# Two-layer cross attention on one core: the first norm of x moved to GpSimd, the last tile's end in halves, and a new written order

## Chip, cores and metric

One core of a Trainium2 chip. The metric is the device time of one execution in microseconds (us), median of several runs. 0.3% of this kernel is 1.0 us.

## What is computed

x is 16 tiles of 128 tokens by 256, the context 16 tiles of 128 by 192, all in fp32. Two layers follow each other, both with 16 heads of 16 columns:

```python
# layer 0
q = layernorm(x, ln1) @ Wq;  k, v = split(layernorm(ctx, ln2) @ Wkv)
x = x + softmax(q k^T / 4) v @ Wproj + bproj
x = x + gelu(layernorm(x, ln3) @ W1 + b1) @ W2 + b2        # 256 -> 1024 -> 256
# layer 1
q = rotate(rmsnorm(x) @ wq);  k, v = split(ctx @ wkv);  k = rotate(k)
x = x + softmax(4 * unit(q) unit(k)^T) v @ wout
```

Each tile attends to its own context tile alone. Products are kept near fp32 accuracy by splitting an operand into a rounded part (`hi`) and the remainder (`lo`), and adding three products.

## The kernel before

The kernel is written for each engine by itself: one list of calls for TensorE (`pe`), VectorE (`dve`), ScalarE (`act`), GpSimd (`pool`) and SyncE (`sp`), unrolled over tiles t (0 to 15) and pairs of tiles p. Each engine works through its list in the written order. The calls are small functions (`statistics(3)`, `keys_a(1, bank_y)`) that wait on semaphores and issue one to a few instructions; between them TensorE's list has further waits for the PSUM banks. Eight banks exist: four score banks (`banks_s`) and `bank_o`, `bank_y`, `bank_t`, `bank_qk`, which all other results pass through.

**Loads.** SyncE loads x and context of tiles 0 and 1 (`load_x`, `load_ctx`, L243 to L249), then waits for the layer-0 key and value weights (`wkv_loaded`, L255), which ScalarE's queue loads in three transfers after the small vectors and Wq (L567 to L571). Then SyncE loads tiles 2 and 3, bproj and Wproj, and the later tiles; `load_x(t)` waits until tile t-4 is normalised.

**Stage A, layer-0 attention (about 13 to 140 us).** Per tile: `statistics` on VectorE (four instructions, L2198 to L2208), `inverse_std` on GpSimd (four, L318 to L331, one a power of -0.5), then `normalise` on VectorE for x (L2210 to L2216) and `normalise_context` on ScalarE (L597). Per pair: TensorE transposes (`rows_T`, `context_T`, four each), ScalarE and VectorE split (`rows_hi`/`rows_lo`, `context_hi_a`/`context_lo_a`), TensorE multiplies (`queries_a` 12 matmuls, `keys_a` and `values_mm_a` 10 each), ScalarE copies out (`queries_out_a`, `keys_out_a`, `values_out_a`). Per tile again: keys are masked in two halves (`masked_first` on ScalarE, `masked_second` on GpSimd, L354), and the scores are made twice in the same four banks. First scores (`scores_a`, L1216, 16 matmuls) serve the row maxima (`maxima`, L2233, VectorE); these are split, transposed and spread (`maxima_hi`, `maxima_lo`, `maxima_T`, `maxima_rows`). Turned scores (`scores_turned`, L1234, 16 matmuls, and `shifted`, L1243, four) overwrite the banks with the maxima taken off, and ScalarE takes the exponentials (`exps_a`, L659, two halves). TensorE then weights the values (`weighted_first`, `weighted_second`, 16 short matmuls each), ScalarE copies (`out_T`), TensorE transposes back (`back`), VectorE divides (`heads_out`), and transposes, splits, `project` (six matmuls) and `residual` end the tile. First scores of tile t+1 are made before the turned scores of tile t. `residual_bias` on GpSimd adds bproj to x once x is normalised.

**Head.** TensorE makes bias products from the raw weights (`query_bias`, `kv_bias`, `proj_bias`), with unused transposes between (`idle`). VectorE copies them out (`kv_bias_out`); `keys_out_a(0)` and `values_bias` wait for that.

**Later.** From about 140 us the MLP (`up_b`, L1326, `down_b`, L1337) runs with layer 1's keys and values mixed in, from 262 us layer 1's attention. `split_wkv`, `w1_lo_part`, `w2_hi_part`, `w2_lo_part` and `context_hi`/`context_lo` on GpSimd prepare operands. The last tile ends with `weighted(31)`, `out_T(31)`, `back(31)`, `heads_out(31)`, `normed(31)`, `out_hi(31)`, `out_lo(31)`, `project(31)`, `residual(31)` and its store.

## Time and profile before

| | us |
|---|---|
| runs | 341.33, 341.97, 341.09; median 341.33 |
| profiled execution, its own time | 343.29 |
| its span on the core | 341.5 |
| TensorE matmul busy | 330.3 (97%) |
| VectorE / ScalarE / GpSimd busy | 266.7 / 230.6 / 193.2 |
| mean granted TensorE clock | 0.992 of 2.4 GHz |

The span is the profiled part of one execution; 1.8 us of its time lie around it. Engines overlap, so their busy times don't add up. PE is TensorE's matmuls, PEld its weight loads, DVE VectorE, ACT ScalarE, POOL GpSimd, SP SyncE; SPq and ACTq are issues of transfers by SyncE and ScalarE. An arrow `<-` between tiles reads output from input; in brackets stands how long the engine was idle before and what released it. A matmul group's printed time includes the last one's way through the array, so the next group starts before it ends.

### The profile page before, as it was taken

How to read it: one execution, taken by the hardware profiler on the slowest of the kernel's cores; microseconds unless marked ns; L12 is line 12 of the kernel's file. 1: busy time of each engine (PE TensorE's matmuls, PEld its weight loads, DVE VectorE, ACT ScalarE, POOL GpSimd, SP SyncE). 2: the span in 40 equal slices, each digit the busy share in tenths (PEclk: the TensorE clock that was granted, in tenths of full speed). 3: DMA queues.
4: the chain of work that ended last, by engine and by line, in shares of the span. 5: the costliest groups of instructions: out<-in, count | busy, mean ns of one | idle time of the engine just before them, and what ended most of it. 6: DMA issues, size and time to landing. Idle time of an engine off the chain costs nothing.

```text
span 341.5 us, 10106 instructions
## 1 busy us (share of the span) xinstructions
PE 330.3 (97%) x3929; PEld 295.5 (87%) x3929; DVE 266.7 (78%) x586; ACT 230.6 (68%) x422; POOL 193.2 (57%) x200
## 2 busy tenths in 40 slices
PE   7899999999999999999999999999998999999995
PEld 7877876888778887899999999999998998888884
DVE  2969989988998669778788788666579989887643
ACT  3568876787775653885736665655678867789871
POOL 3585675886542202635857987493662799647100
PEclk9899999999999999999999999999999999999998
DMA  5667411110020000100000010000000000010101
GB/s 155 200 207 234 138 33 31 33 34 2 3 94 2 3 3 2 33 3 0 3 31 2 0 33 3 31 2 32 2 2 0 3 2 33 17 36 33 50 33 63
DMA packets 13007, 13.79 MB, mean 40 GB/s; under 512 B 1440, under 2 KB 12192, under 8 KB 12960
## 3 DMA queue, kind: packets, MB, share of 16 engines
q1 hardware_dynamic: 12240, 12.34, 11.4%
q10 hardware_dynamic: 720, 0.80, 0.8%
q8 instruction: 32, 0.52, 0.7%
q14 instruction: 15, 0.12, 0.1%
HBM read 11.04 MB, written 2.10 MB: 38 GB/s over the span
## 4 chain that ended last, share of the span: by engine, by line
PE 81%; DVE 6%; issue 4%; POOL 3%; ACT 2%; DMA 1%; ACTq 1%; POOLq 0%; DVEq 0%
PE banks_s L1326 12%; PE bank_y L1121 5%; PE banks_s L1216 5%; PE banks_s L1234 4%; PE banks_s L1393 4%; PE bank_o L1121 4%; PE bank_t L1337 4%; PE bank_y L1337 3%; PE bank_t L1121 3%; PE bank_o L1135 2%; PE bank_y L1135 2%; PE bank_o L1266 2%; PE bank_qk L1337 2%; PE bank_o L1337 2%; DVE row_max L2233 2%
## 5 line engine op out<-in xcount | busy, mean ns | idle before, releaser
L436 POOL TENSOR_TENSOR norm_q_inv<-norm_q_min,minus_half 128x32 f32<-128x32 f32 x8 | 43.8, 5476 | 21.0 <-DVE norm_q_min L2416 19.4
L424 POOL TENSOR_TENSOR norm_k_inv<-norm_k_min,minus_half 128x32 f32<-128x32 f32 x8 | 44.5, 5566 | 12.8 <-DVE norm_k_min L2383 12.7
L659 ACT ACTIVATE PT<-banks_s 128x1024 f32<-128x1024 f32 x32 | 31.0, 1023 | 15.7 <-PE banks_s L1243 15.7
L2233 DVE TENSOR_REDUCE row_max<-banks_s 128x8 f32<-128x1024 f32 x32 | 37.6, 1218 | 4.3 <-PE banks_s L1216 4.0
L703 ACT ACTIVATE W_s<-banks_s,small_t 128x256 f32<-128x256 f32 x60 | 25.2, 471 | 20.1 <-PE banks_s L1326 20.0
L1326 PE MATMUL banks_s<-lnT_hi,W_hi 128*128 128x256 f32 x120 | 34.4, 287 | 0.0
L1326 PE MATMUL banks_s<-lnT_hi,W_lo 128*128 128x256 f32 x120 | 33.9, 283 | 0.0
L1326 PE MATMUL banks_s<-lnT_lo,W_hi 128*128 128x256 f32 x120 | 33.9, 283 | 0.0
L685 ACT ACTIVATE PT<-banks_s 128x1024 f32<-128x1024 f32 x32 | 31.2, 1024 | 3.6 <-PE banks_s L1393 3.6
L712 ACT ACTIVATE hT_hi<-W_s 128x512 fp32r<-128x512 f32 x32 | 20.0, 632 | 15.8 <-PE bank_y L1337 10.1
L389 POOL TENSOR_TENSOR x_all<-x_all,b_row 128x256 f32<-128x256 f32 x16 | 12.4, 794 | 27.2 <-DVE b_xn L2316 25.4
L354 POOL TENSOR_TENSOR masked<-qkT,small_t 128x512 f32<-128x512 f32 x16 | 16.4, 1042 | 16.0 <-ACT qkT L634 15.4
L2327 DVE TENSOR_TENSOR hT_lo<-W_s,hT_hi 128x512 fp32r<-128x512 f32 x32 | 21.3, 688 | 3.9 <-ACT hT_hi L712 3.7
L1326 PEld LDWEIGHTS banks_s<-lnT_hi,W_lo 128*128 128x128 f32 x120 | 23.0, 191 | 0.0
L1326 PEld LDWEIGHTS banks_s<-lnT_lo,W_hi 128*128 128x128 f32 x120 | 23.0, 191 | 0.0
L1326 PEld LDWEIGHTS banks_s<-lnT_hi,W_hi 128*128 128x128 f32 x120 | 23.0, 191 | 0.0
L1216 PE MATMUL banks_s<-masked,qkT 32*128 32x256 f32 x256 | 18.3, 400 | 0.8 <-DVE row_max L2233 0.5
L1234 PE MATMUL banks_s<-masked,qkT 32*128 32x256 f32 x256 | 18.3, 400 | 0.4 <-DVE row_max L2233 0.4
L343 POOL TENSOR_TENSOR x_all<-x_all,bproj_row 128x256 f32<-128x256 f32 x16 | 11.6, 734 | 9.3 <-DVE xn L2216 9.3
L1393 PE MATMUL banks_s<-W_hi,keysT 32*128 32x256 f32 x256 | 15.6, 301 | 0.0
L1216 PEld LDWEIGHTS banks_s<-masked,qkT 32*128 32x128 f32 x256 | 11.6, 184 | 4.5 <-ACT PT L659 1.9
L1234 PEld LDWEIGHTS banks_s<-masked,qkT 32*128 32x128 f32 x256 | 11.6, 184 | 3.3 <-DVE row_max L2233 1.2
(375 smaller groups left out, 1088.6 us busy)
## 6 DMA issues: line engine op xcount, KB each, us to landing
x_all<-in_x SPq DMA_DIRECT2D x16, 128.0 KB, 2.2
ctx_in<-in_ctx_wide SPq DMA_DIRECT2D x16, 128.0 KB, 2.5
W_s<-in_L_xattn_W SPq DMA_DIRECT2D x2, 1024.0 KB, 7.8
ctx_in<-in_ctx_T SPq DMA_DIRECT2D x8, 256.0 KB, 2.6
out<-x_all SPq DMA_DIRECT2D x16, 128.0 KB, 1.7
W_s<-in_L_xattn_Wq ACTq DMA_DIRECT2D x1, 256.0 KB, 3.4
W_s<-in_L_xattn_Wkv ACTq DMA_DIRECT2D x1, 256.0 KB, 4.5
W_s<-in_L_xattn_Wkv ACTq DMA_DIRECT2D x2, 128.0 KB, 4.8
```

Of the source, the lines that this page charges most:

```text
L424: nc.gpsimd.tensor_tensor(norm_k_inv[:, :], norm_k_min[:, :], minus_half[:, :], ALU.pow).then_inc(c_kinv, 1)
L436: nc.gpsimd.tensor_tensor(norm_q_inv[:, :], norm_q_min[:, :], minus_half[:, :], ALU.pow).then_inc(c_qinv, 1)
L659: nc.scalar.activation(PT[:, t % 2, 2 * h:2 * h + 2, :], banks_s[:, 2 * h:2 * h + 2, :], ACT.Exp, scale=HD ** -0.5).then_inc(a_exped, 1)
L685: nc.scalar.activation(PT[:, t % 2, 2 * h:2 * h + 2, :], banks_s[:, 2 * h:2 * h + 2, :], ACT.Exp, scale=HD ** 0.5).then_inc(c_exped, 1)
L703: last = nc.scalar.activation(hT[:, m, :], bank[:, in_pair(k, 256)], ACT.Gelu, bias=b1_cols[:, m:m + 1])
L1121: last = mm(out, a[:, x, k, :], b[:, y, k, :], start=k == n == 0, stop=k == 1 and n == 2)
L1216: last = mm(bank_s[g][:, in_pair(k, 2 * TOK)], qkT[quad(g), p % 2, k, cols], masked[quad(g), t % MASKS, KT + k, :, :], start=True, stop=True)
L1234: mm(bank_s[g][:, in_pair(k, 2 * TOK)], qkT[quad(g), p % 2, KT + k, cols], masked[quad(g), t % MASKS, k, :, :], start=k == 0, stop=False)
L1326: last = mm(bank[:, in_pair(m % 2, 256)], w[:, k, 128 * m:128 * m + 128], act_T[:, k, :], start=k == n == 0, stop=k == KT - 1 and n == 2)
L1337: last = mm(bank[:, 0:C1], h[:, m, 128 * j:128 * j + 128], w[:, m, :], start=m == n == 0, stop=m == HM - 1 and n == 2)
L1393: last = mm(bank_s[g][:, in_pair(k, 2 * TOK)], keysT[quad(g), a, k, in_pair(t, TOK)], masked_q[b][quad(g), p % 2, k, :, in_pair(j, TOK)], ...
L2233: v.tensor_reduce(row_max[:, 8 * h:8 * h + 8], banks_s[:, 2 * h:2 * h + 2, :].rearrange("p n (r k) -> p (n r) k", k=TOK), AX.X, ALU.max).t ...
```

## The change

1. `normalise(t)` moves from VectorE to GpSimd, as one `tensor_scalar` of 128x256. `statistics(t)` on VectorE now also waits until tile t-2 is normalised.
2. The three transfers of the key and value weights move from ScalarE's queue to SyncE's, behind the loads of tiles 0 and 1.
3. For the last tile (31), the steps from the values' weighting to the projection are done in two halves of eight heads, in two banks each.
4. All engines' lists are reordered, and the four banks are given out anew.

```diff
@@ SyncE @@
             load_ctx(1)
+            sp.dma_start(Wkv_s[:, 0, :], Wkv[0:128, :]).then_inc(wkv_loaded, LOADED)
+            for half in (slice(0, C2B), slice(C2B, 128)):
+                sp.dma_start(Wkv_s[half, 1, :], Wkv[128:C2, :]).then_inc(wkv_loaded, LOADED)
             sp.wait_ge(wkv_loaded, 3 * LOADED)
@@ ScalarE @@
-            act.dma_start(Wkv_s[:, 0, :], Wkv[0:128, :]).then_inc(wkv_loaded, LOADED)
-            for half in (slice(0, C2B), slice(C2B, 128)):
-                act.dma_start(Wkv_s[half, 1, :], Wkv[128:C2, :]).then_inc(wkv_loaded, LOADED)
@@ GpSimd (removed from VectorE, where it was v.tensor_scalar) @@
+            def normalise(t):
+                j = t % 2
+                pool.wait_ge(a_rstd, t + 1)
+                pool.wait_ge(a_stats, 2 * t + 1)
+                wait(pool, a_xT, t // 2)
+                nc.gpsimd.tensor_scalar(xn[:, j, :], tile_of(t), mean_var[:, j, 0:1], rstd[:, j, 0:1], ALU.subtract, ALU.mult)\
+                    .then_inc(a_xn, 1)
@@ VectorE, statistics(t) @@
             wait(dve, a_shift, t - 1)
+            wait(dve, a_xn, t - 1)
@@ GpSimd's new list begins @@
+            inverse_std(0) normalise(0) inverse_std(1) normalise(1) inverse_std(2) normalise(2)
+            inverse_std(3) normalise(3) values_bias(0) masked_second(0) masked_second(1)
+            residual_bias(0) residual_bias(1) residual_bias(2) residual_bias(3) inverse_std(4)
+            masked_second(2) masked_second(3) normalise(4) residual_bias(4) inverse_std(5)
+            normalise(5) residual_bias(5) inverse_std(6) normalise(6) residual_bias(6)
...
@@ VectorE's new list begins @@
+            statistics(0) wq_lo_a(0) wq_lo_a(1) statistics(1) query_bias_out(0, bank_o)
+            wkv_lo_a(0) wkv_lo_a(1) statistics(2) rows_lo(0, bank_o) context_lo_a(0, bank_t)
+            statistics(3) statistics(4) wproj_lo(0) kv_bias_out(0, bank_y) statistics(5)
+            rows_lo(1, bank_o) proj_bias_out(0, bank_t) context_lo_a(1, bank_y) maxima(0)
+            maxima_hi(0) maxima_lo(0) maxima_rows(0, bank_y) maxima(1) maxima_hi(1) maxima_lo(1)
+            statistics(6) maxima_rows(1, bank_o) statistics(7) rows_lo(2, bank_y) statistics(8)
+            context_lo_a(2, bank_t) maxima(2)
...
@@ TensorE's list, head, without the waits for banks @@
-            rows_T(0) context_T(0) idle(7) queries_a(0) keys_a(0) rows_T(1) values_mm_a(0)
-            proj_bias(0) scores_a(0) context_T(1) queries_a(1) scores_a(1) keys_a(1) maxima_T(0)
-            values_mm_a(1) scores_turned(0) shifted(0) context_T(2) rows_T(2) maxima_T(1)
-            weighted_first(0) scores_a(2) weighted_second(0) queries_a(2) back(0) scores_turned(1)
+            rows_T(0) context_T(0) idle(8) queries_a(0) keys_a(0) values_mm_a(0) rows_T(1)
+            context_T(1) proj_bias(0) scores_a(0) queries_a(1) keys_a(1) values_mm_a(1)
+            maxima_T(0) scores_a(1) scores_turned(0) shifted(0) maxima_T(1) rows_T(2)
+            context_T(2) weighted_first(0) queries_a(2) scores_a(2) weighted_second(0)
+            rows_T(3) back(0) scores_turned(1)
...
@@ TensorE's list, end @@
-            weighted_first(31) weighted_second(31) project(29) normed(30) back(31) project(30)
-            normed(31) project(31)
+            weighted_first(31) weighted_second(31) project(29) normed(30) back_half(0)
+            back_half(1) project(30) normed_half(0) normed_half(1) project_half(0) project_half(1)
@@ one of the halved steps, on VectorE @@
+            def heads_half(h, bank):
+                o, part = bank[:, :].rearrange("p (h d) -> p h d", h=H), slice(H // 2 * h, H // 2 * h + H // 2)
+                dve.wait_ge(o_back, 2 * NB + h)
+                dve.wait_ge(on_ready, 2 * NB - 1)
+                v.reciprocal(row_sums_inv[:, part], o[:, part, HD]).then_inc(recip, 1)
+                dve.wait_ge(recip, 2 * NB + h)
+                dve.wait_ge(on_transposed, 2 * NB - 1)
+                v.tensor_tensor(heads(on[:, in_pair(h, TOK)], H // 2), o[:, part, 0:HD], each(row_sums_inv[:, part], H // 2, HD), ALU.mult).then_inc(on_ready, 1)
@@ VectorE's new list ends @@
+            out_lo(30) heads_half(0) heads_half(1) residual(30) out_lo_half(0) out_lo_half(1) residual(31)
```

## Rows read from the trace of the kernel before

**Rows 1.** Windows: us, busy us (instructions) per engine, TensorE clock, DMA share, GB/s

```profile
13.00:140.00 127.00, 124.41 (x1574) 100.87 (x1572) 110.76 (x255) 87.31 (x150) 69.35 (x119) 0.99 0.20 63
...
140.00:260.00 120.00, 119.31 (x1052) 117.74 (x1046) 88.96 (x177) 77.89 (x165) 80.37 (x51) 1.00 0.03 10
```

**Rows 2.** Timeline, score banks: start us, us, work [idle before <-releaser]

```profile
20.11 1.15 PE L1216 MATMUL banks_s<-masked,qkT 32*128 32x256 f32 x16
...
23.74 1.15 PE L1216 MATMUL banks_s<-masked,qkT 32*128 32x256 f32 x16 [0.47 <-DVE row_max L2233]
...
25.00 2.35 DVE L2233 TENSOR_REDUCE row_max<-banks_s 128x8 f32<-128x1024 f32 x2
...
27.51 1.15 PE L1234 MATMUL banks_s<-masked,qkT 32*128 32x256 f32 x16
...
28.97 1.92 ACT L659 ACTIVATE PT<-banks_s 128x1024 f32<-128x1024 f32 x2
...
30.94 1.15 PE L1216 MATMUL banks_s<-masked,qkT 32*128 32x256 f32 x16
...
131.36 1.15 PE L1216 MATMUL banks_s<-masked,qkT 32*128 32x256 f32 x16 [0.19 <-ACT PT L659]
```

**Rows 3.** Timeline, TensorE work between the score groups

```profile
32.58 1.70 PE L1121 MATMUL bank_y<-xT_r,Wq_r 128*128 128x256 f32 x12
...
56.00 0.63 PE L1256 MATMUL bank_o<-PT,vals 128*17 128x128 f32 x16
...
57.44 0.63 PE L1288 MATMUL bank_o<-ident,oT 128*128 128x128 f32 x4 [0.81 <-ACT oT L673]
```

**Rows 4.** VectorE groups, whole span: shapes, xcount | busy us, mean ns | idle before

```profile
L2308 DVE SCALAR_TENSOR_TENSOR b_xn<-x_all,b_mean_var,ln_rows 128x256 f32<-128x256 f32 x16 | 8.1, 545 | 2.2 <-PE bank_o L1313 2.2
...
L2216 DVE TENSOR_SCALAR xn<-x_all,mean_var,rstd 128x256 f32<-128x256 f32 x16 | 6.8, 432 | 0.0
```

**Rows 5.** Timeline, VectorE at 97 to 99 us

```profile
97.12 1.91 DVE L2308 SCALAR_TENSOR_TENSOR b_xn<-x_all,b_mean_var,ln_rows 128x256 f32<-128x256 f32 x2
...
98.95 0.68 DVE L2221 TENSOR_TENSOR xT_r<-bank_t,xT_r 128x512 fp32r<-128x512 f32 x1
```

**Rows 6.** GpSimd groups, whole span, columns as in rows 4

```profile
L389 POOL TENSOR_TENSOR x_all<-x_all,b_row 128x256 f32<-128x256 f32 x16 | 12.4, 794 | 27.2 <-DVE b_xn L2316 25.4 <-ACT qkT L634 1.8
...
L403 POOL CAST wkv_r<-wkv_s 128x256 fp32r<-128x256 f32 x4 | 1.6, 404 | 0.0
```

**Rows 7.** Timeline of the head, issues of loads and two waits

```profile
1.67 0.49 ACTq L569 DMA_DIRECT2D W_s<-in_L_xattn_Wkv  x1
...
2.12 0.43 SPq L249 DMA_DIRECT2D ctx_in<-in_ctx_wide  x1
...
11.59 0.69 PE L1129 MATMUL bank_t<-ident,xn 128*128 128x128 f32 x4 [1.19 <-DVE xn L2216]
...
11.62 0.43 SPq L249 DMA_DIRECT2D ctx_in<-in_ctx_wide  x1
...
15.00 0.43 DVE L2203 BATCH_NORM_STATS2 stats<-x_all 128x6 f32<-128x256 f32 x1 [0.19 <-DMA ctx_in<-in_ctx_wide]
```

**Rows 8.** Chain that ended last, the head: start us, us, what

```profile
2.75 4.97 DMA W_s<-in_L_xattn_Wkv
```

**Rows 9.** Busy time in windows of 1 us, columns as in rows 1

```profile
12.00:13.00 1.00, 1.00 (x8) 1.00 (x7) 1.00 (x7) 0.60 (x1) 0.57 (x3) 0.54 0.83 282
...
14.00:15.00 1.00, 1.00 (x6) 1.00 (x6) 0.81 (x2) 0.32 (x1) 0.97 (x4) 0.50 0.72 236
...
15.00:16.00 1.00, 1.00 (x9) 1.00 (x8) 1.00 (x5) 0.72 (x2) 0.20 (x2) 0.75 0.17 49
```

**Rows 10.** Timeline, end of the span

```profile
335.54 0.25 DVE L2274 RECIPROCAL row_sums_inv<-bank_o 128x16 f32<-128x16 f32 x1
...
336.97 0.39 ACT L679 ACTIVATE onT_r<-bank_o 128x256 fp32r<-128x256 f32 x1 [1.81 <-PE bank_o L1295]
...
338.94 0.42 DVE L2290 TENSOR_TENSOR x_all<-x_all,bank_o 128x256 f32<-128x256 f32 x1 [1.13 <-PE bank_o L1121]
```

More of the change, by code:

```diff
@@ new lines, in _ @@
+            pe.wait_ge(onT_lo, 14)
+            project(13, bank_o)
+            pe.wait_ge(a_max_rows, 16)
+            values_mm(1, bank_t)
+            pe.wait_ge(a_exped, 32)
+            up_b(0, 1, bank_s[0])
+            pe.wait_ge(res_ready, 14)
+            back(14, bank_o)
+            pe.wait_ge(oT_ready, 15)
+            weighted_first(15, bank_qk)
+            weighted_second(15, bank_qk)
+            pe.wait_ge(on_ready, 15)
+            normed(14, bank_o)
+            up_b(0, 2, bank_s[1])
@@ L2541, in _ @@
-            statistics(14)
-            maxima_rows(8, bank_y)
-            residual(4, bank_t)
-            normalise(14)
+            heads_out(6, bank_o)
+            rows_lo(6, bank_t)
+            statistics(15)
+            maxima_rows(8, bank_o)
+            centre_b(0)
+            residual(5, bank_qk)
             maxima(9)
-            out_lo(5, bank_qk)
+            out_lo(6, bank_o)
             maxima_hi(9)
             maxima_lo(9)
-            heads_out(6, bank_o)
-            statistics(15)
+            normalise_b(0)
@@ L2789, in _ @@
+            out_lo(21, bank_o)
             heads_out(22, bank_qk)
@@ L2805, in _ @@
             heads_out(26, bank_qk)
[L2806 to L2808 removed]
+            out_lo(25, bank_t)
+            queries_out_lo(7, bank_y)
+            residual(25, bank_t)
             heads_out(27, bank_qk)
```

1741 lines of the change are left out of this document (875 added, 866 removed).

## The prediction

> **What bounds the kernel now.** I read the stage windows first. From 13 to 140 us (the first layer's attention, "stage A") TensorE is busy 124.4 of 127 us and VectorE 110.8; from 140 to 260 us TensorE is busy 119.3 of 120 [rows 1]. So after 140 us a gain has to come from TensorE work or from the last microseconds, and stage A is where waits can go.
>
> In stage A the four score banks form a ring that I read off the timeline [rows 2]: first scores (1.15 us), maxima on VectorE (2.35), turned scores with the shift (27.51 until the exponentials start at 28.97, 1.4), exponentials on ScalarE (1.92), then the next first scores. With about 0.05 us between two steps a turn takes 7.0 us. From the first scores of tile 2 (30.94) to those of tile 15 (131.36) 13 turns took 100.4 us, 7.72 each, 9.3 us over that floor. TensorE works on other matmuls while VectorE (2.42 us with its gaps) and ScalarE (2.04) hold the banks. I priced these from starts: 12 matmuls 1.5 us, so 10 are 1.25; 16 short ones 0.5; four transposes 0.35 to 0.5 (a row's last 0.15 to 0.2 us is pipeline) [rows 3]. Added up over the written order of before, what exceeds its slot comes to 6.3 us; that is work and stays. The other 3.0 us are waits for VectorE or ScalarE.
>
> VectorE's part in them: the normalisation that is moved is 16 x 432 ns = 6.8 us; its group of two-tile reads L2308 takes 545 ns an instruction [rows 4]. At 97 us two of these took 1.91 us, 0.8 more than twice the mean, and the split of xT_r behind them started at 98.95 only [rows 5].
>
> **The change part by part.** (1) **Normalisation to GpSimd.** VectorE loses 16 x 0.43 us, 6.1 us of it in stage A, 0.4 of some 7.7 us a tile. GpSimd gains 16 instructions that no row shows. With one wide input it is nearest to the cast of 256 columns (404 ns); the two-input one of that size took 794 ns [rows 6]. I take 0.5, as it also fetches two scalars: 8 us, range 6.5 to 12.7. GpSimd is busy 69 of 127 us [rows 1], so there is room for the sum, though not at each place. New waits: statistics(t) on VectorE waits for xn of tile t-2, behind which stand maxima and all splits; rows_T waits as before, now on GpSimd's queue, where the masks and residual_bias stand too. residual_bias no longer waits for VectorE. Of the 3.0 us of waits I take back 2.0, range 0 to 3.0: VectorE's load falls from 87 to 82%, and not all waits were its.
>
> The GPSIMD Engine Reference of the Trainium skill (section 4.1) holds that elementwise work belongs on VectorE, two-input operations being about twice as slow on GpSimd and one-input ones near line rate. By its second half the moved instruction would be at the 0.43 of VectorE and the sum 0.1 to 0.2 us better at most.
>
> (2) **Weights' loads.** The three issues leave ScalarE's queue, the first at 1.67 us, and go behind SyncE's fourth at 2.12 [rows 7], so each is 0.5 to 0.7 us later. The last landed at 7.72 [rows 8]. x and context of tile 1 go ahead and land sooner, which hides nothing that waits now. If the engines' traffic sets the landing, nothing moves; if the issue does, 0.7 later. I take 0.4: 8.15. SyncE holds its next loads until then. TensorE's bias matmuls took 2.3 us behind the landing and end at 10.4 now; rows_T(0), which waited for xn until 11.59 [rows 7], starts there: xn of tile 1 (statistics at 7.0, GpSimd's reciprocal root, 0.5 us) is ready at 9.2 to 9.8. That is 1.1 us gained.
>
> (3) **The clock in the head.** TensorE waited 1.2 us for xn [rows 7], and the granted clock from 12 to 16 us was 0.54, 0.50, 0.50 (two windows alike, one stands) and 0.75, so mostly 1.2 GHz [rows 9]; before that it was full. Without the wait I take it to stay at 2.4 GHz, so queries_a(0) takes 1.5 us in place of 2.05.
>
> (4) **But what is gained is not kept to the loop.** The written order puts kv_bias_out on VectorE behind statistics(3), statistics(4) and wproj_lo(0). Context of tile 4 was issued at 11.62 and VectorE waited for it until 15.00 [rows 7]; xn now releases that load 0.4 us sooner and the weights hold it 0.4 later, so it lands at 14.9. Adding 0.9 for statistics(4), 0.65 for wproj_lo, 0.15 for the copy: 16.65. ScalarE's keys_out_a(0) 0.85, values_out_a 0.6, rows_hi(1) 0.6 and masked_first(0) 0.75 follow in its order: 19.5, first scores of tile 0 at 19.6 in place of 20.11 [rows 2]. Then all of queries, keys and values of pair 1 (1.5 + 1.25 + 1.25 us) stand between first scores 0 and 1: those of tile 1 start at 24.75 (23.74 before). Turned scores 0 follow them directly, with no work between: TensorE idles for the maxima, 2.4 us, to 28.35 (27.51 before). Exponentials to 31.75, but the first half lets weighted_first(0) run, and queries_a(2), now ahead of first scores 2, ends at 32.8: tile 2 at 32.8 in place of 30.94, **+1.86 us**, with queries_a(2) done. From there to tile 15 its excess over the slots is 5.7 us in place of 6.3, **-0.6**; the same work has then been done in both. Behind tile 14's shift one half of weighted is moved back: **-0.3**.
>
> (5) **The last tile in halves.** Before: reciprocal 335.54, product, transposes, ScalarE's copy 336.97 (0.39), VectorE's remainder, six matmuls, residual 338.94 [rows 10]. In halves the reciprocal still waits for out_lo(30) at 335.54. A half of an operation of 0.39 to 0.42 us costs about 0.28 (VectorE: 0.42 for 256 columns [rows 10], 0.68 for 512 [rows 5]). The halves follow each other at 0.3: transposes 336.45 and 336.65, copies to 337.4, remainders to 337.7, last three matmuls done at 338.4: **-0.5**, range -0.1 to -0.9.
>
> (6) **The rest of the order** (second half of the kernel, banks renamed). It moves values_mm and keys_c forward where TensorE is full anyway: 0, by the cover of 119.3 of 120 us; without it, up to 1 us either way.
>
> **Sum:** +1.86 - 0.6 - 0.3 - 2.0 - 0.5 = -1.5 us. The profiled execution took 343.29 us (span 341.5), so 341.8; it lies 2.0 above the median, and from the median of 341.33 it is **339.8 us**. A measurement here tells 0.3%, 1.0 us, from no change.
>
> **The rivals.** *GpSimd comes late, slower.* The place: normalise(4), (5), (6), behind masked_second(2) and (3) at 24 to 32 us; rows_T(2), and statistics(8) in front of the maxima of tile 2, wait on them, by my timeline with only 0.3 us to spare. At 0.8 us in place of 0.5 three of them make 0.9, less 0.3 spare: +0.6; and a VectorE that stands in a statistics wait takes none of the 2.0 back: 339.8 + 0.6 + 2.0 = 342.4. It decides from about 0.6 us an instruction. For it speaks the 794 ns, against it the 404 ns [rows 6] and GpSimd's idle time. Chance 0.23.
>
> *VectorE and GpSimd collide, no change.* The 0.8 us lost at 97 us [rows 5] fell beside a 1.5 us subtraction on GpSimd. If each of the 16 new ones costs VectorE 0.25, 4 of the 6.8 us freed are gone, and with them 1.2 to 1.5 of the 2.0: 341.2. Chance 0.14. SBUF — State Buffer of the Trainium skill (section "Who interferes with whom") gives a mechanism: a VectorE instruction with two SBUF inputs contends with a GpSimd one that reads SBUF. By that rule the row's loss is explained, and the removed normalisation, one wide input, gave way to nothing.
>
> *The clock falls in the new gap.* TensorE idles 2.4 us after tile 1's first scores, longer than the 1.2 us ahead of the low stretch [rows 7, 9]. The same stretch costs (0.46 + 2 x 0.50 + 0.25) = 1.7 us: 341.5. Chance 0.10.
>
> *All waits go.* Relief of 3.0, and the weights no later (0.4): 338.4, or 337.5 with the later stages' 0.9. Chance 0.13.
>
> **How the numbers follow.** My forecast has 0.40, its own range 338.8 to 340.8. The range 337.4 to 342.8 takes in the ends of GpSimd's price, of the landing and of part 6. Faster: three quarters of 0.40, 0.13 and a little of the rest, 0.46; same 0.23; slower 0.31.
>
> **What would show it.** Right: xn on GpSimd at 0.4 to 0.6 us; rows_T(0) near 10.4; clock 1.00 from 12 to 16 us; first scores of tiles 0, 1, 2 near 19.6, 24.8, 32.8; tile 15 near 130.3 to 131; residual to store shorter by 0.5. Wrong: xn above 0.7 us, statistics waiting for GpSimd, a half-rate stretch after 28 us, or tile 2's first scores before 31.

## The result, and the profile after

The changed kernel took a median of 351.10 us in 4 runs (348.48 to 352.84) beside 341.33 us for the kernel before: the ratio is 1.0277 with the interval 1.0207 to 1.0346. It is slower by 2.8%, where 339.8 us (337.4 to 342.8) was forecast. The profiled execution took 351.86 us with a span of 349.8, against 343.29 and 341.5. The profiled execution of the kernel before is one of its longer ones: of nine others, taken beside e17, four with a mean granted clock of 1.000 took 341.06 to 342.09 us and five at 0.992 to 0.995 took 342.01 to 342.88.

First TensorE's timeline, which answers to [rows 2] and [rows 7]: L1168 turns rows of x, L1255 is the first scores, L1273 the turned scores, L1160 the queries, L1174 the keys.

```profile
10.61 0.63 PE L1168 MATMUL bank_o<-ident,xn 128*128 128x128 f32 x4 [0.59 <-POOL xn L347]
...
24.10 1.15 PE L1255 MATMUL banks_s<-masked,qkT 32*128 32x256 f32 x16
27.72 1.15 PE L1273 MATMUL banks_s<-masked,qkT 32*128 32x256 f32 x16 [2.48 <-DVE row_max L2288]
...
30.52 1.09 PE L1168 MATMUL bank_y<-ident,xn 128*128 128x128 f32 x4 [1.05 <-POOL xn L347]
...
33.37 2.83 PE L1160 MATMUL bank_y<-xT_r,Wq_r 128*128 128x256 f32 x12
36.13 1.15 PE L1255 MATMUL banks_s<-masked,qkT 32*128 32x256 f32 x16
...
42.86 0.58 PE L1174 MATMUL bank_o<-yT_r,Wkv_r 128*128 128x256 f32 x1 [1.73 <-DVE on L2332]
...
140.11 0.50 PE L1255 MATMUL banks_s<-masked,qkT 32*128 32x256 f32 x4 [0.19 <-ACT PT L684]
```

From such starts the 8.3 us of span can be laid out. The first scores of tiles 0, 1, 2, 3 and 15 start at 18.89, 24.10, 36.13, 46.60 and 140.11 us, before at 20.11, 23.74, 30.94, 38.45 and 131.36. So the head comes 1.22 earlier; the step to tile 1 loses 1.58, that to tile 2 4.83, that to tile 3 2.96; the twelve steps from there together 0.60; and what follows tile 15's scores gains 0.45. Nearly the whole loss lies in 22 us of the span. The 1.22 of the head can't be credited to the change: e4, e7, e8, e10, e17 and e18 below have the same written order up to tile 0's first scores, and these start at 19.23 to 20.15 us there.

What became slow is one row of GpSimd's groups (columns as in rows 4), where 0.5 us had been taken:

```profile
L347 POOL TENSOR_SCALAR xn<-x_all,mean_var,rstd 128x256 f32<-128x256 f32 x16 | 20.1, 1254 | 0.0
```

Who waited for `xn`, from the view of that tile (us in all, times); in the kernel before no line of VectorE's waited for it:

```profile
who waited for it (us, times):
  ACT xT_r L633: 5.3, 6
  DVE stats L2266: 2.8, 5
```

GpSimd's timeline ahead of tile 2 (L355 is residual_bias, L334 the shift of the context's norm):

```profile
25.91 1.22 POOL L347 TENSOR_SCALAR xn<-x_all,mean_var,rstd 128x256 f32<-128x256 f32 x1
27.21 0.72 POOL L355 TENSOR_TENSOR x_all<-x_all,bproj_row 128x256 f32<-128x256 f32 x1
...
28.98 0.19 POOL L334 TENSOR_TENSOR y_shift<-minus_mean,rstd 128x1 f32<-128x1 f32 x1
29.14 1.22 POOL L347 TENSOR_SCALAR xn<-x_all,mean_var,rstd 128x256 f32<-128x256 f32 x1
```

and ScalarE's:

```profile
29.20 0.60 ACT L622 ACTIVATE yn<-ctx_in,y_shift,rstd 128x256 f32<-128x256 f32 x1 [3.27 <-POOL y_shift L334]
29.71 1.00 ACT L684 ACTIVATE PT<-banks_s 128x1024 f32<-128x1024 f32 x1
31.64 0.60 ACT L633 ACTIVATE xT_r<-bank_y 128x512 fp32r<-128x512 f32 x1 [0.93 <-PE bank_y L1168]
32.13 1.02 ACT L684 ACTIVATE PT<-banks_s 128x1024 f32<-128x1024 f32 x1
```

The two halves of tile 0's exponentials belong together, as at 28.97 in [rows 2]. Here the first stands behind a norm of the context that waits for GpSimd's shift. Of ScalarE's 3.27 us of idle time this costs the exponentials about 0.6: TensorE had the turned scores with their shift ready at 29.10 us, and the first half starts at 29.71. The second half stands behind a copy of the turned rows of pair 2, which wait for norm 5, done at 30.37 us, and starts at 32.13. The queries of pair 2 stand ahead of tile 2's first scores and take 2.83 us instead of 1.7, because the clock has fallen. The windows (columns as in rows 1) of stage A, of the next stage, and of two microseconds behind TensorE's idle stretch:

```profile
13.00:140.00 127.00, 118.81 (x1447) 94.81 (x1445) 100.89 (x224) 83.89 (x144) 80.86 (x127) 0.96 0.21 59
140.00:260.00 120.00, 119.89 (x1087) 117.33 (x1088) 90.22 (x186) 73.80 (x161) 78.40 (x55) 1.00 0.04 12
29.00:30.00 1.00, 0.46 (x5) 0.14 (x1) 0.51 (x2) 0.80 (x2) 1.00 (x2) 0.56 0.65 205
30.00:31.00 1.00, 0.48 (x3) 0.52 (x4) 0.68 (x3) 0.71 (x1) 0.92 (x2) 0.50 0.01 3
```

In stage A TensorE is busy for 5.6 us less of the same 127 us than in [rows 1]; the next stage is as full as it was. The granted clock was at half rate, 1.2 GHz, from 29.1 to 36.0 and from 42.8 to 46.2 us.

At tile 3 something else shows, on VectorE's timeline:

```profile
39.74 1.22 DVE L2299 CAST max_cols<-row_max 128x16 fp32r<-128x16 f32 x1
41.00 1.19 DVE L2304 TENSOR_TENSOR max_cols<-row_max,max_cols 128x16 f32<-128x16 f32 x1
...
42.38 0.42 DVE L2332 TENSOR_TENSOR on<-bank_o,row_sums_inv 128x256 f32<-128x256 f32 x1
```

and on GpSimd's at the same time:

```profile
39.66 3.72 POOL L372 TENSOR_TENSOR W_lo<-W_s,W_hi 128x512 fp32r<-128x512 f32 x3 [0.74 <-ACT W_hi L615]
```

The two small operations take 0.17 to 0.18 us at tile 0, with no subtraction of weights beside them. Behind them stands `on`, for which the keys of pair 2 wait until 42.86 us, ahead of tile 3's first scores.

The end, for [rows 10], on VectorE: first reciprocal of a half, and the last residual.

```profile
344.19 0.20 DVE L2344 RECIPROCAL row_sums_inv<-bank_t 128x8 f32<-128x8 f32 x1
...
347.24 0.42 DVE L2360 TENSOR_TENSOR x_all<-x_all,bank_o 128x256 f32<-128x256 f32 x1 [0.93 <-PE bank_o L1440]
```

3.05 us between these starts, against 3.40 before.

### The profile page after: what moved, and what is told of

It reads as the page before. It is cut to its first block, busy times and chain, and to the rows that moved or that the text cites. A ratio compares the mean times of both kernels' runs of the same rounds, so it can differ in the third digit from the quotient of the medians.

```text
span 349.8 us, 10121 instructions
## 1 busy us (share of the span) xinstructions
PE 333.7 (95%) x3930; PEld 296.9 (85%) x3930; DVE 264.3 (76%) x573; ACT 231.9 (66%) x424; POOL 211.4 (60%) x216
## 4 chain that ended last, share of the span: by engine, by line
PE 70%; DVE 4%; issue 2%; POOL 2%; ACT 1%; POOLq 0%; DVEq 0%; ACTq 0%
PE banks_s L1365 13%; PE bank_t L1376 6%; PE banks_s L1452 4%; PE bank_y L1376 4%; PE bank_o L1160 4%; PE bank_y L1160 4%; PE bank_o L1376 3%; PE banks_s L1273 3%; PE bank_y L1174 2%; PE banks_s L1255 2%; PE bank_o L1305 2%; PE bank_t L1160 2%; PE bank_y L1176 2%; DVE row_max L2288 1%; PE bank_qk L1305 1%
## 5 line engine op out<-in xcount | busy, mean ns | idle before, releaser
L740 ACT ACTIVATE W_s<-banks_s,small_t 128x256 f32<-128x256 f32 x62 | 26.0, 472 | 19.5 <-PE banks_s L1365 19.3
L1365 PE MATMUL banks_s<-lnT_hi,W_hi 128*128 128x256 f32 x124 | 35.4, 285 | 0.0
L1365 PE MATMUL banks_s<-lnT_lo,W_hi 128*128 128x256 f32 x124 | 35.1, 283 | 0.0
L1365 PE MATMUL banks_s<-lnT_hi,W_lo 128*128 128x256 f32 x124 | 35.1, 283 | 0.0
L2397 DVE TENSOR_TENSOR hT_lo<-W_s,hT_hi 128x512 fp32r<-128x512 f32 x32 | 22.1, 703 | 4.8 <-ACT hT_hi L749 4.5
L401 POOL TENSOR_TENSOR x_all<-x_all,b_row 128x256 f32<-128x256 f32 x16 | 12.9, 825 | 19.6 <-DVE b_xn L2386 19.6
L1365 PEld LDWEIGHTS banks_s<-lnT_hi,W_lo 128*128 128x128 f32 x124 | 23.8, 192 | 0.0
L1273 PE MATMUL banks_s<-masked,qkT 32*128 32x256 f32 x256 | 18.3, 400 | 3.4 <-DVE row_max L2288 3.3
L347 POOL TENSOR_SCALAR xn<-x_all,mean_var,rstd 128x256 f32<-128x256 f32 x16 | 20.1, 1254 | 0.0
L1255 PE MATMUL banks_s<-masked,qkT 32*128 32x256 f32 x256 | 18.3, 400 | 0.2 <-ACT PT L684 0.2
L1273 PEld LDWEIGHTS banks_s<-masked,qkT 32*128 32x128 f32 x256 | 11.6, 184 | 7.0 <-DVE row_max L2288 5.1
L1376 PE MATMUL bank_t<-W_hi,hT_hi 128*128 128x256 f32 x56 | 16.3, 291 | 0.0
L423 POOL CAST ctxT_r<-ctx_in 128x512 fp32r<-128x512 f32 x8 | 4.9, 611 | 18.4 <-issue 9.1
```

The costliest lines, as they stand in the source:

```text
L740: last = nc.scalar.activation(hT[:, m, :], bank[:, in_pair(k, 256)], ACT.Gelu, bias=b1_cols[:, m:m + 1])
L1255: last = mm(bank_s[g][:, in_pair(k, 2 * TOK)], qkT[quad(g), p % 2, k, cols], masked[quad(g), t % MASKS, KT + k, :, :], start=True, stop=True)
L1273: mm(bank_s[g][:, in_pair(k, 2 * TOK)], qkT[quad(g), p % 2, KT + k, cols], masked[quad(g), t % MASKS, k, :, :], start=k == 0, stop=False)
L1365: last = mm(bank[:, in_pair(m % 2, 256)], w[:, k, 128 * m:128 * m + 128], act_T[:, k, :], start=k == n == 0, stop=k == KT - 1 and n == 2)
L1376: last = mm(bank[:, 0:C1], h[:, m, 128 * j:128 * j + 128], w[:, m, :], start=m == n == 0, stop=m == HM - 1 and n == 2)
L2397: v.tensor_tensor(hT_lo[:, part(u), :], hT[:, part(u), :], hT_hi[:, part(u), :].bitcast(fp32), ALU.subtract)\
```

## The experiments

"Old order" is the written order of the kernel before on all engines, "new order" that of the changed one. The last columns are starts of first scores in the profiled execution, in us. Each ratio is to runs of the kernel before on the same chip, whose median was 341.31 to 342.09 us in these batches.

| run | norm of x | order | median us | ratio to before [interval] | t0 | t1 | t2 | t3 | t15 |
|---|---|---|---|---|---|---|---|---|---|
| before | VectorE | old | 341.33 | | 20.11 | 23.74 | 30.94 | 38.45 | 131.36 |
| after | GpSimd 1224 ns | new | 351.10 | 1.0277 [1.0207, 1.0346] | 18.89 | 24.10 | 36.13 | 46.60 | 140.11 |
| e1 | GpSimd 396 ns | new | 349.64 | 1.0217 [1.0173, 1.0260] | 19.47 | 24.67 | 34.53 | 44.20 | 139.56 |
| e2 | GpSimd 612 ns | new | 349.10 | 1.0199 [1.0156, 1.0242] | 19.23 | 24.43 | 33.54 | 44.07 | 138.18 |
| e3 | VectorE | new | 356.69 | 1.0415 [1.0379, 1.0451] | 19.16 | 24.37 | 34.95 | 45.55 | 144.91 |
| e4 | GpSimd 1224 | new, gap filled | 348.00 | 1.0169 [1.0145, 1.0192] | 20.12 | 25.31 | 35.44 | 42.94 | 136.81 |
| e5 | GpSimd 1224 | old | 346.17 | 1.0123 [1.0097, 1.0148] | 20.91 | 24.53 | 31.71 | 40.09 | 134.15 |
| e6 | VectorE | old, queue, halves | 342.06 | 1.0007 [0.9986, 1.0028] | 18.70 | 22.33 | 29.54 | 37.03 | 129.92 |
| e7 | GpSimd 1224 | new, w1 later | 355.62 | 1.0403 [1.0373, 1.0433] | 19.78 | 24.98 | 35.91 | 43.10 | 143.71 |
| e8 | GpSimd 1224 | new, scores first | 348.82 | 1.0205 [1.0172, 1.0237] | 19.23 | 24.43 | 33.71 | 42.94 | 136.65 |
| e9 | GpSimd 396 | old | 341.75 | 0.9998 [0.9981, 1.0015] | 18.40 | 22.02 | 29.22 | 36.71 | 129.58 |
| e10 | GpSimd 1224 | new, keys after | 352.45 | 1.0313 [1.0266, 1.0361] | 20.12 | 24.21 | 39.10 | 47.01 | 140.62 |
| e11 | GpSimd 1224 | new, e8 + e10 + w1 last | 356.83 | 1.0423 [1.0381, 1.0464] | 19.32 | 23.40 | 36.44 | 45.60 | 142.91 |
| e12 | GpSimd 396 | as e11 | 349.72 | 1.0235 [1.0198, 1.0273] | 19.01 | 23.09 | 34.38 | 43.29 | 137.69 |
| e13 | GpSimd 1224 | new, biases later | 349.18 | 1.0216 [1.0187, 1.0244] | 20.69 | 25.89 | 35.42 | 42.65 | 136.79 |
| e14 | GpSimd 1224 | e13 + turned early | 351.94 | 1.0285 [1.0250, 1.0319] | 21.94 | 27.13 | 34.17 | 43.08 | 140.65 |
| e15 | GpSimd 396 | as e14 | 348.98 | 1.0208 [1.0181, 1.0234] | 19.96 | 25.17 | 32.21 | 41.12 | 137.50 |
| e16 | GpSimd 1224 | old, biases later, queue, halves | 347.19 | 1.0173 [1.0140, 1.0207] | 19.21 | 22.84 | 30.15 | 42.11 | 135.48 |
| e17 | GpSimd 1224 | new, lists repaired | 349.96 | 1.0224 [1.0202, 1.0246] | 20.15 | 25.36 | 32.39 | 41.30 | 139.06 |
| e18 | GpSimd 1224 | e17, norms 10, 11 first | 349.18 | 1.0216 [1.0192, 1.0240] | 19.25 | 24.45 | 31.48 | 40.39 | 136.37 |

### e1 and e2: a shorter instruction in the new order

```diff
-nc.gpsimd.tensor_scalar(xn[:, j, :], tile_of(t), mean_var[:, j, 0:1], rstd[:, j, 0:1], ALU.subtract, ALU.mult)
+nc.gpsimd.tensor_copy(xn[:, j, :], tile_of(t))                                  # e1
+nc.gpsimd.tensor_tensor(xn[:, j, :], tile_of(t), <mean, broadcast>, ALU.subtract)  # e2
```

> The changed kernel, in which the normalisation on GpSimd is replaced by a plain copy of the same 128x256 tile; mean and deviation of x are left out. The trace of the changed kernel shows the moved instruction at 1254 ns, where I had taken 500; the copy should take about 0.4 us, close to my 0.5. Theory A (the instruction's length makes GpSimd late): the time falls to about 340, within 1.5 us of my forecast of 339.8, and the first scores of tile 3, at 46.6 us in the changed kernel and 38.45 before, come at 38 to 40. Rival B (the new written order costs it, above all the empty stretch behind the first scores of tile 1 and the half-rate clock after it, whatever GpSimd takes): 347 or more.

> The changed kernel, in which the normalisation on GpSimd is replaced by a subtraction of the mean alone (two inputs, one of them broadcast); the factor is left out. About 0.75 us an instruction, between the copy and the 1.25 us. Theory A: between the two, 342 to 345, nearer to the copy if GpSimd's queue has slack, nearer to 351 if it has none. Rival B: 347 or more, as the copy.

The rows of `xn` in the view of that tile (ns: least, median, most; first and last start in us), e1:

```profile
L347 POOL COPY xn<-x_all x16: 392/396/398, 7.6 to 96.2; 128x256 f32<-128x256 f32 x16
```

e2:

```profile
L347 POOL TENSOR_TENSOR xn<-x_all,mean_var x16: 608/612/617, 6.7 to 94.7; 128x256 f32<-128x256 f32 x16
```

Below the 0.5 us of the forecast, e1 is still 7.6 us slower than before. The length alone is not the cause; of the 8.75 us at tile 15 it gave back 0.55 (1.13 counted from tile 0's first scores). e2, between the two lengths, took 349.10 us. Theory A fell in both, and rival B's 347 us or more held. The intervals of e1, e2 and the changed kernel overlap, so these runs don't resolve what the length costs in this order.

### e3: the norm back on VectorE, new order

The function and its 16 calls go back to VectorE's list, at places near those of before that I chose; everything else is the changed kernel.

> The changed kernel with the normalisation back on VectorE (16 instructions of 0.43 us, placed near statistics of tile t+2 in its list); every other list, the loads' queue and the halves stay as changed. Theory A: 340 to 343, since GpSimd is relieved of 20 us and VectorE only takes 6.8 back in a list that was not made for it. Rival B: 347 or more.

With e11 this is the slowest, 14.6 us over before (342.05 in its batch), and rival B's range held. The new order thus seems to need the time that the move frees on VectorE; but the places of the 16 calls were chosen by hand, and no run tells their share from that. One norm stands out on VectorE's timeline:

```profile
25.08 1.26 DVE L2254 TENSOR_SCALAR xn<-x_all,mean_var,rstd 128x256 f32<-128x256 f32 x1
```

and beside it on GpSimd's:

```profile
24.15 2.04 POOL L357 TENSOR_TENSOR masked<-qkT,small_t 128x512 f32<-128x512 f32 x2 [0.39 <-ACT qkT L634]
```

The median of e3's 16 norms is 414 ns.

### e4: TensorE's idle stretch filled

```diff
 scores_a(1)
+pe.wait_ge(a_bp, 1)
+for n in range(22): nc.tensor.transpose(bank_t[:, 0:128], ident[:, :], ident[:, :])   # unused
 pe.wait_ge(a_maxed, 4)
```

> The changed kernel with 22 unused transposes on TensorE in the empty stretch between the first scores of tile 1 and the turned scores of tile 0. They compute nothing that is used. If the half-rate clock from 28.8 us on comes of that stretch and costs as much as I priced (1.7 us), the granted clock stays at 1.00 there and the time falls by 1 to 2 us, to 349 to 350. If GpSimd's lateness alone sets the pace (theory A), the clock may stay up but the time changes by less than 0.5 us. If they only add work: slower by up to 0.5.

Windows of e4, columns as in rows 1; against the same two windows of the changed kernel the clock stays at 1.00:

```profile
29.00:30.00 1.00, 1.00 (x21) 0.86 (x20) 0.97 (x5) 0.00 (x0) 1.00 (x4) 1.00 0.87 254
30.00:31.00 1.00, 0.57 (x9) 0.14 (x1) 0.61 (x4) 0.59 (x2) 0.92 (x3) 1.00 0.46 138
```

Useless work made the kernel 3.1 us faster, more than the 1 to 2 us expected. The step to tile 2 fell from 12.03 to 10.13 us and that to tile 3 from 10.47 to 7.50. At tile 3 the maxima's splits also no longer fell beside the weights' subtraction (they take 0.19 and 0.18 us), and e7 below shows that this alone brings the step to 7.19. So the 3.1 us are clock and collision together, and how they divide is not shown.

### e5 and e9: the move alone, old order

```diff
 # GpSimd's list of before, for each t
 inverse_std(t)
+normalise(t)
 # VectorE: its 16 calls go; in statistics(t)
+wait(dve, a_xn, t - 1)
```

> The kernel of before with one edit: the first norm of x on GpSimd, each right behind its inverse deviation, with VectorE's statistics waiting for it; the other engines' written order, the loads and the end stay those of before. Theory A (the written order of the change costs the time, not the 1254 ns on GpSimd): GpSimd's length makes a few waits near the first tiles only, 341 to 345 us, with first scores of tile 15 within 3 us of before's 131.36. Rival B (GpSimd's length holds the statistics and the turned inputs in any order): 348 us or more, first scores of tile 15 at 137 us or later.

> The kernel of the old order with the norm on GpSimd, in which the 1224 ns instruction is a plain copy of about 0.40 us (mean and deviation left out), so that only its length is changed against the old order's 346.17 us. Theory A (in the old order the move costs what the instruction is longer than the 0.5 us of the prediction): 341.5 to 343 us, within 1.5 us of before. Rival B (the two waits that the move adds, GpSimd for the turned pair and VectorE's statistics for GpSimd, cost it, whatever the length): 344.5 to 346.5 us.

e5 lies between its two theories: tile 15 is 2.79 us later, as A had it, and the time 1.2 us above A's range. e9 is A's. Together they settle the length in the old order: at 396 ns the move costs nothing that the runs can tell, at 1224 ns 4.4 us. From tile 1 to 7 e9 makes the steps of before to 0.02 us. So neither rival about the added waits as such holds; and against e1 (same instruction, new order) the new order costs 7.9 us. In these 7.9 are the queue and the halves, which e6 puts at nothing, and the banks given out anew, which no run separates from the order.

### e6: loads' queue and halves alone

The diff of the change for the three loads of Wkv and for the last tile, on the kernel before.

> The kernel of before with the loads of Wkv on SyncE's queue and the last tile's end in halves, and nothing else. The steps of the prediction put the halves at -0.5 us (-0.1 to -0.9) and the loads at 0 (-0.3 to +0.3): 340.8 us beside 341.3. If the halves' extra instructions cost what they save, within 0.2 us of before. The profile is to show the last projection's start against the last weighted product, as a check of the first, and the clock and start of the first scores for the second.

No difference that the runs can tell. In the trace reciprocal to last residual is 3.06 us (334.07 to 337.13) for 3.40, so the halves' 0.34 us is there, and it is the part of the change that does what it was forecast to.

### e7: weights' subtractions later

```diff
 inverse_std(8)
-w1_lo_part(0), (1), (2)
 masked_second(4)
 masked_second(5)
+w1_lo_part(0), (1), (2)
 w1_lo_part(3)
 normalise(8)
```

> The changed kernel with its three w1_lo_part (0 to 2) on GpSimd behind masked_second(4) and (5), as far back as part 3, so that they no longer lie beside the maxima's splits of tile 2. Theory A (the GpSimd subtractions slow the two small VectorE operations from 0.17 to 1.2 us each, and heads_out(0), keys_a(2) and first scores of tile 3 are late by that): both operations below 0.3 us, first scores of tile 3 1.5 to 2.5 us nearer to those of tile 2, 348.5 to 349.5 us. Rival B (the delay is hidden by another wait, or the half clock runs on): within 0.5 us of the changed kernel's 351.1.

Timeline of VectorE:

```profile
39.51 0.17 DVE L2299 CAST max_cols<-row_max 128x16 fp32r<-128x16 f32 x1
39.72 0.17 DVE L2304 TENSOR_TENSOR max_cols<-row_max,max_cols 128x16 f32<-128x16 f32 x1
...
52.35 0.43 DVE L2266 BATCH_NORM_STATS2 stats<-x_all 128x6 f32<-128x256 f32 x1 [3.82 <-POOL xn L347]
```

and of GpSimd:

```profile
46.01 5.00 POOL L372 TENSOR_TENSOR W_lo<-W_s,W_hi 128x512 fp32r<-128x512 f32 x4
51.00 1.21 POOL L347 TENSOR_SCALAR xn<-x_all,mean_var,rstd 128x256 f32<-128x256 f32 x1
```

Theory A's first half holds: without the subtraction beside them the splits are back at 0.17 us, and the step to tile 3 is 7.19 us for 10.47. But nothing of this is kept. Norm 8 stands behind the four subtractions in both kernels. In e7 GpSimd starts them only behind the masked copies, and norm 8 starts at 51.00 us, as in the changed kernel (50.91), while VectorE is now 3.5 us ahead. Its statistics wait 3.82 us for that norm, tile 3's splits stand behind these, and the clock is at half rate from 54.8 to 61.7 us. The kernel loses 4.5 us more and falls in neither range. The added wait of VectorE, harmless in e9, is what such a place costs.

### e8: scores ahead of queries

```diff
 # ScalarE
-rows_hi(2, bank_y)
 exps_a_second(0)
+rows_hi(2, bank_y)
 # TensorE
-queries_a(2, bank_y)
 scores_a(2)
+queries_a(2, bank_y)
```

> The changed kernel with two places of its written order exchanged: on ScalarE the second exponentials of tile 0 ahead of rows_hi(2), on TensorE the first scores of tile 2 ahead of queries_a(2). Theory A (the order makes scores of tile 2 wait for rows_T(2), rows_lo(2) and the queries, which GpSimd's norm makes late): first scores of tile 2 at 31.5 to 33.5 us instead of 36.13, and 347.5 to 350 us. Rival B (what is gained there is lost at tile 3, since the keys, maxima and clock are late all the same): first scores of tile 3 within 0.7 us of 46.60, and 350.3 to 351.5 us.

Theory A: both steps shorten (9.28 and 9.23 us), though tile 2, at 33.71 us, lies 0.2 outside its range. The median is 2.3 us lower, but the interval of the ratio just overlaps that of the changed kernel. The clock is at half rate from 27.6 to 34.4 us here too.

### e10, e11, e12: repairs that made it worse

e10 moves keys and values of pair 1 and maxima_T(0) behind scores_a(1), as in the old order, and maxima_rows(0) behind maxima(1). e11 adds e8 and puts all w1_lo_part behind residual_bias(10); e12 is e11 with the copy.

> The changed kernel with the keys and values of pair 1 and the turning of tile 0's maxima on TensorE behind the first scores of tile 1, where the old order has them, and VectorE's maxima_rows(0) behind maxima(1). Nothing else is changed. Theory A (the idle stretch at 25.2 to 27.7 us comes of the written order, and the half clock at 28.8 us of it): no half clock from 28 to 36 us, first scores of tile 2 1 to 3 us earlier than 36.13, 347.5 to 349.5 us, near the 348.0 us of the kernel in which unused transposes filled the stretch. Rival B (the turned scores of tile 0 come later by the moved work, 2 us, and take it back): 350 to 352 us.

> The changed kernel with three repairs of its written order together: keys and values of pair 1 behind the first scores of tile 1; exponentials and first scores of tile 2 ahead of rows_hi(2) and queries_a(2); all four w1_lo_part on GpSimd behind residual_bias(10). The norm stays on GpSimd at 1224 ns. Theory A (the order is what costs over the 346.17 us of the old order with the same norm): 345 to 347 us, no half clock after 28 us, maxima's splits of tile 2 at 0.17 us each. Rival B (later places of the new order cost as much by themselves): 348 us or more, with first scores of tile 15 at 136 us or later.

> The three repairs with the norm's instruction as a plain copy of about 0.40 us on GpSimd (mean and deviation left out). Theory A (order and length together are the whole loss): 341 to 343.5 us. Rival B (a remainder that neither explains, in the order of tiles 4 to 15): 344.5 us or more; first scores of tile 3 near 38.5 us and the distance from there to tile 15 (92.91 us in the kernel of before) 95 us or more.

The idle stretch ahead of tile 0's turned scores is gone, yet the step to tile 2 is 14.89 us in e10: TensorE now idles 4.11 us for norm 5, at 30.3 to 34.4, and the clock is at half rate from 34.6 to 38.0 us. Theory A of all three fell. e10 is 0.45 us above rival B's range too; e11 and e12 are in rival B's, but in e12 tile 3's first scores come at 43.29 us and not near 38.5, so the loss is not where that rival had it. The traces say why. ScalarE in e12:

```profile
31.08 0.60 ACT L622 ACTIVATE yn<-ctx_in,y_shift,rstd 128x256 f32<-128x256 f32 x1 [2.40 <-POOL y_shift L334]
31.59 1.92 ACT L684 ACTIVATE PT<-banks_s 128x1024 f32<-128x1024 f32 x2
```

and GpSimd:

```profile
26.64 2.04 POOL L366 TENSOR_TENSOR masked<-qkT,small_t 128x512 f32<-128x512 f32 x2 [3.06 <-ACT qkT L659]
28.62 0.40 POOL L347 COPY xn<-x_all 128x256 f32<-128x256 f32 x1
...
30.86 0.19 POOL L334 TENSOR_TENSOR y_shift<-minus_mean,rstd 128x1 f32<-128x1 f32 x1
```

GpSimd's list has masked_second(2) and (3) ahead of norm 4. They wait for keys 1; later keys make norm 4, then inverse deviation 5 late; ScalarE's norm of context 5 waits for its shift; and tile 0's exponentials, whose bank TensorE had ready at 28.2, stand behind that. The new order has the keys early, and GpSimd's list needs them there. e11 and e12 differ in the instruction alone: in this order 1224 in place of 396 ns cost 7.1 us.

### e13 to e16: GpSimd's list by need

e13 changes GpSimd's list alone:

```diff
 inverse_std(2)
-normalise(2)
 inverse_std(3)
+normalise(2)
 normalise(3)
...
 masked_second(1)
-residual_bias(0), (1), (2), (3)
 inverse_std(4)
+normalise(4), inverse_std(5), normalise(5)
 masked_second(2)
 masked_second(3)
+residual_bias(0) to (3), then 6 and 7 likewise
```

e14 also turns pair 2's rows and context between scores_a(1) and scores_turned(0), with their copies ahead of the exponentials, and has e8's exchange on TensorE. e15 is e14 with the copy. e16 is e13's list in the old order, with queue and halves.

> The changed kernel with one edit, on GpSimd's list alone: inverse deviations and norms of tiles 3, 4 and 5 as early as their inputs are there, and residual_bias(0) to (7), which nobody needs before the first residual sum, behind them. Theory A (GpSimd's own order is what makes the turned inputs of pair 2 late: four residual biases at 19.50 to 22.32 us and two masked copies stand ahead of norm 4, and norm 5 ends at 30.37 us): norm 5 ends by 25 us, the turned inputs of pair 2 (30.52 us) and the first scores of tile 2 (36.13 us) come 1.5 us and 2 to 4 us earlier, 346 to 349 us. Rival B (TensorE's idle stretch at 25.2 to 27.7 us and its half clock hold tile 2): 349.5 to 351.5 us.

> As the one before, and the turned inputs and context of pair 2 on TensorE in the idle stretch between the first scores of tile 1 and the turned scores of tile 0, with their splits ahead of the exponentials of tile 0 on ScalarE and VectorE, and the first scores of tile 2 ahead of queries_a(2). Theory A (the whole loss lies in tiles 1 to 3, in what TensorE waits for there): first scores of tile 2 at 30.5 to 32 us, no half clock after 28 us, 342 to 344.5 us. Rival B (each wait removed gives way to the next, as in the three repairs before): 347 us or more.

> As the one before, with the norm on GpSimd as a plain copy of about 0.40 us (mean and deviation left out). Theory A (with GpSimd's list in this order its length is covered): within 1 us of the one before. Rival B (the length still costs, as the 4.4 us between 346.17 and 341.75 us in the old order): 2 us or more below it.

> The old written order with the norm on GpSimd at 1224 ns, the loads of Wkv on SyncE's queue and the end in halves, and GpSimd's list as in the two before (norms early, residual biases late). Theory A (the 4.2 us of the norm in the old order are its places behind other work of GpSimd): 341.5 to 343.5 us. Rival B (the length itself, 1224 ns beside 432 ns on VectorE, costs): 345 to 346.5 us.

Norm 5 ends at 26.1 us in e13 (25 expected), no half clock is left, and the steps to tiles 2 and 3 are 9.53 and 7.23 us; e14's step to tile 2 is 7.04, shorter than before's 7.20. But the swap of norm 2 and inverse deviation 3 holds statistics(4) for 2.67 us, and first scores 0 come 1.80 and 3.05 us later (not all of it by the swap: e17, without it, is still 1.26 later, and so far the head scatters by itself); e14 loses another 4.1 against the changed kernel at tiles 4 and 5, where w1_lo_part stands ahead of norm 8. e15 is 3.0 us below e14: the length is not covered. By their times e13 lies between its two theories, and rival B held for e14 and e15. In e16, whose steps to tiles 1 and 2 are those of before within 0.11 us, the step to tile 3 is 11.96. At 347.19 us e16 is beyond rival B's range and 1.0 above e5, without this list. ScalarE's timeline names the place:

```profile
34.92 0.60 ACT L622 ACTIVATE yn<-ctx_in,y_shift,rstd 128x256 f32<-128x256 f32 x1 [1.36 <-POOL y_shift L334]
35.43 0.58 ACT L698 ACTIVATE oT<-bank_qk 128x512 f32<-128x512 f32 x1
```

out_T(0), for which TensorE waits 2.68 us, stands behind the norm of context 7. That one waits for inverse deviation 7 on GpSimd, which stands behind norm 6 (32.42 to 33.65 us) and, until 31.2 us, the four residual biases put ahead of it.

### e17 and e18: the places left

e17 is e14 without the swap in the head, with norms 6 to 9 ahead of biases and of w1_lo_part, and statistics 6 and 7 earlier on VectorE. e18 puts norms 10 and 11 ahead too, and w1_lo_part behind the other weights' work.

> The changed kernel with the norm on GpSimd at 1224 ns and its first 18 tile steps as they are (norm 2 ahead of inverse deviation 3 again), then GpSimd's list by need: norms 4 to 9 ahead of the residual biases and of w1_lo_part, the masked copies between; the turned inputs and context of pair 2 in TensorE's idle stretch, as in e14; VectorE's statistics 6 and 7 ahead of maxima_rows(0) and (1). Theory A (the loss of 9.1 us is places in the lists of tiles 1 to 5, above all what stands on GpSimd ahead of the norms, and the length is coverable): first scores of tile 0 near 18.9, tile 2 near 31.1, tile 3 near 39, no wait of VectorE's statistics over 1 us after 20 us, 342 to 345 us. Rival B (each wait gives way to the next one, since GpSimd has no time left beside 1224 ns a tile): 347 us or more.

> As e17, with the one place that the trace of e17 shows left: norms 10 and 11 on GpSimd ahead of all w1_lo_part, of masked_second(6) and (7) and of the first splits of wkv; three w1_lo_part behind the last w2_lo_part (GpSimd idles there from 73.6 to 78.0 us) and the last behind residual_bias(15). Theory A: the step from tile 5 to 6 falls from 12.08 to 8.3 us (8.34 in the changed kernel) without the half clock at 64 us, first scores of tile 15 at 135.3, 345.5 to 346.5 us, that is the time of the old order with this norm (346.17). Rival B (the next place takes it back): first scores of tile 15 at 138 us or later, 348.5 us or more.

e17 is 4.80 us ahead of the changed kernel at tile 5 and loses it in the next step (12.08 us), on TensorE:

```profile
63.99 0.78 PE L1168 MATMUL bank_qk<-ident,xn 128*128 128x128 f32 x4 [2.71 <-POOL xn L347]
64.70 2.09 PE L1273 MATMUL banks_s<-masked,qkT 32*128 32x256 f32 x16
```

In e18 that step is 7.95 us, as forecast; the steps to tiles 7 to 10 then take 34.23 us for 31.30 in the changed kernel, and the median, 0.8 us lower, is no difference that the runs can tell. Whether the weights' work, now in one stretch there, makes these steps long was not traced. Theory A of both fell on the total. Of its places it had e17's step from tile 0 to 2 (12.24 us for 12.2) and e18's to tile 6; e17's tile 3, at 41.30 us for 39, and e18's tile 15, at 136.37 for 135.3, it had not. The rivals' times held, though e18's tile 15 came before rival B's 138: each place gives way to the next.

## Why the prediction was wrong, point by point

**Step (1), the price of the norm, failed.** The norm was priced at 0.5 us (range 0.40 to 0.79) from the nearest rows, a cast at 404 and a two-input operation at 794 ns [rows 6]. It took 1224 ns, outside both ends: the copy took 396 ns, one subtraction 612, subtraction and multiplication together twice that. In the old order this is 4.4 us (e5, e9). The rival "GpSimd comes late" had the place (norms 4 to 6 behind the masked copies) and the waits right, and its point of decision, 0.6 us, lay on the right side; its 342.4 us was priced with 0.8 us an instruction, and the old order gives 346.17.

**Step (1), the list of waits, was short of one.** It named VectorE's statistics and TensorE's turned rows. It left out the shift that the next inverse deviation gives to ScalarE's norm of the context: it stands behind the norm on GpSimd, and exponentials and out_T stand behind it on ScalarE (3.27 us idle in the changed kernel, which delays the exponentials by 0.6; 3.4 in e12, and out_T in e16).

**The relief of 2.0 us did not come.** The step counted VectorE's freed 6.1 us as waits taken back. In e9, where norms are off VectorE at no cost, the twelve steps from tile 3 to 15 take 92.87 us for 92.91: nothing. Only its head is earlier, by 1.71 us, and its median (341.75) equals that of before (342.03 beside it). The step took waits for VectorE to shrink with its load; from tile 3 on e9 shows none that does.

**Step (2) hit its number by luck.** rows_T(0) starts at 10.61 us, for 10.4. But the weights did not land 0.4 us later: SyncE, which waits for all three transfers, issues its next load at 7.07 us, where the last had landed at 7.72, and the bias products end at 10.0. What TensorE then waits for, 0.59 us, is the term that the step had safe at 9.8: norm 1 on GpSimd, which takes 1.71 us beside VectorE's subtraction of weights (7.83 to 9.36 us):

```profile
8.75 1.71 POOL L347 TENSOR_SCALAR xn<-x_all,mean_var,rstd 128x256 f32<-128x256 f32 x1
```

**Step (3) held in this execution, not in every one.** queries_a(0) takes 1.67 us and the clock is full from 12 to 16 us. In e4 and e10, with the same order up to there, it is at half rate from 11.6 to 15.0 and from 10.8 to 14.1 us, and their first scores 0 come at 20.12. So 18.89, for 19.6, is no proof of step (4)'s account of the head; kv_bias_out comes at 15.49 us there, for 16.65.

**Step (4) failed at tile 2.** First scores 1 at 24.10 (24.75) and turned scores at 27.72 (28.35) were even early; tile 2 came at 36.13 for 32.8. The step had tile 0's exponentials run without a gap and the queries of pair 2 start at about 31.3 us (32.8 less 1.5), with the rows turned and split in time. In their place stood the order on ScalarE, which parts the exponentials, norm 5 at 30.37, so that the queries start at 33.37, and the clock, at which they take 2.83. "-0.6" over the further tiles was +0.60 from tile 3 on, and tile 3 itself added 2.96, through the wait of the keys for `on` and the collision with w1_lo_part, which no step mentions. In the comparison of e1 with e9 the order costs 7.9 us, where +1.86, -0.6 and -0.3 were forecast.

**The rival "VectorE and GpSimd collide"** had the mechanism and not the place: it spread the loss over the norms and priced the whole at 341.2 us. What collided were subtractions of weights with the two splits of one tile, which took 2.07 us too long together; e7 takes this away, and with it the half clock behind it, and the step falls by 3.28 us. That the removed norm gave way to nothing was wrong already for the kernel before. Norm 5 there takes 0.79 us for 0.41, beside a masked copy on GpSimd (27.30 to 29.34 us):

```profile
28.69 0.79 DVE L2216 TENSOR_SCALAR xn<-x_all,mean_var,rstd 128x256 f32<-128x256 f32 x1
```

**The clock was made a rival with 0.10** and priced 1.7 us, for one such stretch. It came, for 6.9 us behind the gap and for 3.4 behind TensorE's wait for `on`, and filling the gap gave back 3.1 together with the collision. Its wrong treatment is that it excluded the other cases: late GpSimd, order and clock added up, as a longer gap is what lateness makes.

**Step (5) held**: -0.35 us for -0.5. **Step (6) held**: after tile 15's scores 209.7 us for 210.1, which is the halves.

The sum in parts, each from runs: length 4.4 us in the old order; order 7.9 at 396 ns (e1, e9) and 4.9 at 1224 ns (after, e5). 4.4 + 7.9 is more than the loss of 9.8: the two meet in the same waits. So the length has no price of its own: it is 1.5 us in the new order (after, e1, with overlapping intervals), 3.0 in e14's (e14, e15), 4.4 in the old and 7.1 in e11's (e11, e12). Which further places of the new order cost the last 5 us of e18 stays open. No run beat the kernel before; e6 and e9 equal it.
